# Routed cross attention: GpSimd's add of the normalised rows waits for the router's products, the second division goes ahead of the third maxima, the last copy ahead of an inverse

## The reference, cut to what matters

```python
qh, kh, vh = split(layernorm(x) @ wq + bq), split(ctx @ wk + bk), split(ctx @ wv + bv)
attn = softmax(einsum('bhqd,bhkd->bhqk', qh, kh) * scale)
x = x + (merge(einsum('bhqk,bhkd->bhqd', attn, vh)) @ wo + bo)
h = layernorm(x)
scores = h @ w_router            # one number for each token
_, idx = top_k(scores, 128)      # of the 512 tokens of the batch
x_sel = take(h, idx)             # goes to the mixture of depths
x = x + ffn(h)                   # ffn(h) is h, but for the chosen rows
```

## Time and profile before

| what | value |
| --- | --- |
| median of three runs (lowest, highest) | 2496.6 us (2495.58, 2496.82) |
| the profiled execution's own time | 2497.47 us |
| its span in the trace | 2495.6 us |
| TensorE busy | 91% of the span, 2259.5 us |
| VectorE, ScalarE, GpSimd busy | 57%, 48%, 30% |
| granted TensorE clock, mean | 0.963 of full speed |
| the stage of the change | about 505 to 815 us of the span |

### The profile page before, as it was taken

How to read it: one execution, slowest core, us unless ns; L and a number is a source line. 1 busy time by engine, 2 the same in 40 slices (tenths; PEclk the granted TensorE clock), 3 DMA queues, 4 the chain that set the end, 5 groups by cost and what they waited for, 6 DMA issues and landing times. The chain is left out here.

```text
span 2495.6 us, 44295 instructions
## 1 busy us (share of the span) xinstructions
PE 2259.5 (91%) x13992; PEld 1433.7 (57%) x13993; DVE 1423.5 (57%) x3651; ACT 1188.6 (48%) x2803; POOL 743.2 (30%) x848
## 2 busy tenths in 40 slices
PE   7999999888886699899999999889985899999998
PEld 5444554454555476643333333255552799999997
DVE  4666666435776354387777777366654534344343
ACT  1666666623432464258777777523322533333332
POOL 3112111043431331233232232054520533333333
PEclk8999999989998899999999999999997899999999
DMA  5343443113221320223333333010009322222221
GB/s 161 103 132 122 132 128 121 60 47 127 72 79 51 83 71 1 70 78 107 94 108 100 99 99 105 33 45 12 9 1 337 102 34 36 35 35 37 33 36 23
DMA packets 160823, 197.00 MB, mean 79 GB/s; under 512 B 27238, under 2 KB 121104, under 8 KB 160528
## 3 DMA queue, kind: packets, MB, share of 16 engines
q1 hardware_dynamic: 145008, 175.47, 22.6%
q0 software_dynamic: 13680, 17.84, 4.4%
q10 hardware_dynamic: 1968, 1.60, 0.4%
HBM read 124.83 MB, written 70.12 MB: 78 GB/s over the span
## 5 line engine op out<-in xcount | busy, mean ns | idle before, releaser
L485 ACT ACTIVATE self_probs<-self_score_ps 128x512 f32<-128x512 f32 (+3 forms) x1024 | 479.5, 516 | 260.1 <-PE self_score_ps L856 150.0
L653 DVE TENSOR_REDUCE self_neg_max<-self_max_ps 128x1 f32<-128x512 f32 x512 | 328.5, 685 | 127.7 <-PE self_max_ps L842 123.9
L842 PE MATMUL self_max_ps<-self_k_stack,self_q_stack 96*128 96x512 bf16 (+3 forms) x1024 | 349.1, 343 | 32.1 <-DVE self_neg_max L650 21.9
L853 PE MATMUL self_score_ps<-self_q_stack,self_k_stack 99*128 99x512 bf16 (+3 forms) x1024 | 345.9, 345 | 14.0 <-ACT self_probs L485 13.7
L2757 ACT ACTIVATE x_stream<-experts_up_ps,experts_bias_now 128x128 f32<-128x128 f32 x568 | 161.9, 368 | 351.0 <-PE experts_up_ps L2969 351.0
L650 DVE CUSTOM_DVE_ANT_0 self_masked<-self_max_ps,self_later 128x128 f32<-128x128 f32 (+3 forms) x512 | 235.0, 488 | 127.7 <-PE self_max_ps L842 120.3
L2969 PEld LDWEIGHTS experts_up_ps<-experts_tileT,x_stream 128*128 128x128 f32 x2272 | 266.8, 193 | 5.2 <-issue 1.6
L2969 PE MATMUL experts_up_ps<-experts_tileT,x_stream 128*128 128x128 f32 x2272 | 267.2, 276 | 1.2 <-DVE x_stream L2879 1.2
L2979 PE MATMUL experts_down_ps<-experts_down,x_stream 128*128 x1136 | 256.8, 379 | 0.0
L853 PEld LDWEIGHTS self_score_ps<-self_q_stack,self_k_stack 99*128 99x128 bf16 x1024 | 99.2, 98 | 248.3 <-ACT self_probs L485 181.4
L867 PE MATMUL self_out_ps<-self_probs,self_values 128*32 128x512 f32 (+3 forms) x2048 | 234.7, 530 | 7.3 <-ACT self_o_raw L471 5.4
(11 more groups left out here) (339 smaller groups left out, 3811.5 us busy)
## 6 DMA issues: line engine op xcount, KB each, us to landing
self_parts_dram<-self_parts SPq DMA_DIRECT2D x64, 384.0 KB, 2.7
self_q_stack<-self_parts_dram SPq DMA_DIRECT2D x384, 64.0 KB, 2.3
self_k_stack<-self_parts_dram SPq DMA_DIRECT2D x360, 64.0 KB, 2.3
self_out_dram<-self_o_raw SPq DMA_DIRECT2D x60, 256.0 KB, 2.2
crossx_out_dram<-crossx_o_raw SPq DMA_DIRECT2D x16, 512.0 KB, 2.7
experts_up<-moe_up_dram SPq DMA_DIRECT2D x8, 1024.0 KB, 9.3
experts_down<-moe_down_dram SPq DMA_DIRECT2D x8, 1024.0 KB, 10.6
self_o_now<-self_out_dram SPq DMA_DIRECT2D x30, 256.0 KB
```

Source lines behind the costliest of these rows:

```text
L485: act.activation(probs[:, i % 8, 0:w], score_ps[:, (16 * n + i) % 3, 0:w], ACT.Exp).then_inc(exp_done, 1)
L653: dve.tensor_reduce(neg_max[:, n % 2, t, h:h + 1], max_ps[:, i % 2, 0:w], AX, ALU.max, negate=True).then_inc(max_read, 1)
L842: last = pe.matmul(max_ps[:, i % 2, 0:w], q_stack[0:ROWS, h, P * t:P * t + P], k_stack[0:ROWS, h, 0:w], start=True, stop=True)
L853: last = pe.matmul(score_ps[:, m % 3, 0:w], k_stack[0:KROWS, head, P * j:P * j + P], q_stack[0:KROWS, head, S - w:S], start=True, stop=not ...
```

## The change

Three edits in the same stage, which change no arithmetic.

GpSimd's add x = x + h of a batch waits, beside h itself (`h_done`), for the four products with the router's row (`scored`). In each pass of ScalarE the inverse of the sums (b-1,1) goes ahead of the copy of the queries (b+2,1), and in each pass of VectorE the division (b-1,1), which needs this inverse, goes ahead of the maxima (b+1,2). After the loop, ScalarE copies out the last half (7,1) before it inverts the sums of (7,0), which wait for a load.

```diff
--- before.py
+++ after.py
@@ -1601,6 +1601,7 @@
                     pool.wait_ge(r_ln_eps, b + 1)
                     pool.tensor_tensor(r_rstd[:], r_var_eps[:], c.minus_half[:, 0:TT], ALU.pow).then_inc(r_ln_rstd, 1)
                     pool.wait_ge(h_done, TT * b + TT)
+                    pool.wait_ge(scored, TT * b + TT)
                     pool.tensor_tensor(c.x[:, b], c.x[:, b], h[:], ALU.add).then_inc(h_added, 1)
 
                 inverse_deviation(0)
@@ -1719,16 +1720,16 @@
                     if next2:
                         queries(b + 2, 0)
                     exponentials(b, 2)
+                    if b >= 1:
+                        inverted(b - 1, 1)
                     if next2:
                         queries(b + 2, 1)
-                    if b >= 1:
-                        inverted(b - 1, 1)
                     copy_out(b, 0)
                     exponentials(b, 3)
                     if b >= 2:
                         chosen_kept(b - 2)
+                copy_out(B - 1, 1)
                 inverted(B - 1, 0)
-                copy_out(B - 1, 1)
                 scores_copied(B - 2)
                 inverted(B - 1, 1)
                 chosen_kept(B - 2)
@@ -1863,10 +1864,10 @@
                         normalise(b - 1, 0)
                     if choice:
                         compare(b - 2, (0, 1))
+                    if b >= 1:
+                        normalise(b - 1, 1)
                     if more:
                         maxima(b + 1, 2)
-                    if b >= 1:
-                        normalise(b - 1, 1)
                     if choice:
                         compare(b - 2, (2, 3))
                         choose(b - 2)
```

## The result

The kernel with all three edits takes 2478.18 us (median of 5, 2473.38 to 2482.36), the one before on the same chip 2495.58 (median of 5, 2492.61 to 2496.82): a ratio of 0.993, 95% interval 0.9916 to 0.9945. The profiled execution took 2478.18 with a span of 2476.3, against a span of 2495.6 before.

What follows compares the result with a forecast made beforehand. TensorE was taken to bound the program, waiting at sr and e and losing clock. Batches 1 to 7 give 1.0, 0, 4.2, 6.0, 4.5, -1.45, 1.0, tail 4.0: 19.25 us, 2496.6 to 2477.6, range 2474 to 2486.

Steps and rivals of the forecast that it cites:

- rival 1: TensorE's clock doesn't come back and it stays partly at half clock; gain 13.5 us, 2483 us; 16 in 100.
- Rival 2: GpSimd's add, copy and bias add run as one 6.9 us piece, blocking VectorE's first division; 2483.5 us; 12 in 100.
- Rival 3: VectorE's second product is slow for its own reason; only the earlier division works; 2492 us; 4 in 100.
- rival 4: Load sets e in batches 3 to 5, merged idle piece costs half clock, 1.7 us each; 2498 us; 3 in 100.
- The stall: VectorE's second router product loses 2.15 us beside GpSimd's add in each of eight batches; holding the add ends it.
- The clock's part: TensorE's slow stretch behind sr in batches 3 to 5 returns to full clock: 5.7 us, bounded by 0 and 5.7.
- Where the stall goes: The add moves beside VectorE's next maxima, first division and comparisons; VectorE wins only 0.6 us in batch 5.
- The division: Moved forward on VectorE, it ends e's 1.00 us wait in batches 1, 3, 4, 5; gives 0.9 in batch 5.
- Pass 2: The gain at sr is waited away at e for a late load: 0 us, bounds -0.5 and 0.3.
- Pass 6: Load sets e; one idle piece of 3.65 us costs half clock: -1.45 us, bounds -1.7 and +0.25.
- Pass 7 and the tail: 1.0 us from batch 7's wait at e, plus 1.85 + 2.15 = 4.0 in the tail.
- Edit 3: Last half's store and loads leave about 3.7 us earlier; worth 0 by itself, 0.3 at most as cover.

Runs made afterwards that it cites:

- run 1: Kernel before with only GpSimd's add of x and h held until the router's products are done; 2482.61 us, ratio 0.9954.
- run 4: Kernel before with GpSimd's add of x and h replaced by a fill of an unused tile; one execution 2480.72 us, stage 237.25.
- run 5: Changed kernel with the inverse back ahead of the last copy, so without the third edit; 2481.68 us, ratio 0.9961.
- run 2: Kernel before with only the second inverse and division moved forward; 2490.01 us, ratio 0.9989.
- run 3: Kernel before with only the last copy put ahead of the inverse; one execution 2487.40 us, stage 250.46.
- run 7: Changed kernel with the next stage's weight loads spread over passes 1 to 6 and their scaling in pass 7; 2474.23 us, ratio 0.9917.
- run 9: Changed kernel with useless TensorE products ahead of e, 30 in pass 2 and 13 in passes 6 and 7, more in the tail; 2468.11 us, ratio 0.988.
- run 6: Changed kernel with useless TensorE products ahead of e, 56 in pass 2 and 24 in passes 6 and 7, more in the tail; 2480.13 us, ratio 0.9931.
- run 11: Changed kernel with 13 useless products in passes 6 and 7, the tail's, and weight loads behind half 0's store in passes 1 to 3; 2465.94 us, ratio 0.9883.
- run 10: Changed kernel with weight loads in passes 1 to 5 and 13 useless products in passes 6 and 7, plus the tail's; 2470.96 us, ratio 0.9897.

## Why the prediction was right

2477.6 was predicted and 2478.18 measured, in the range, with the forecast's own mechanism; rivals 1 to 4 didn't come. But the agreement to 0.6 is luck: the stage gave 16.66 where the sum had 19.25, while 3.57 were gained behind the stage and 0.93 lost ahead of it, where no edit reaches.

**The stall (edit 1): right.** A slow product needed GpSimd's add beside it, shown by run 1 (waits instead) and run 4 (fill instead), both with 424 ns at most. Rival 3 falls with run 4. The clock's part in passes 3 to 5, taken in full, came in full: the granted clock is 1.00 in all three, and run 1 gives 12.23 us in them, wait and clock together, for the 11.9 predicted. The 0.1 more in each pass is the full-clock time from sr to the scores of S, 3.14 for the 3.25 assumed. In these passes rival 1 falls.

**Where the stall goes: right in pass 5.** Division 1.56, ties 1.30 and 1.64 (as before the change), VectorE in at the hand-overs; the comparisons ended 7.3 us behind the products, 7.6 by the prediction. Rival 2's one piece of 6.9 didn't form. The sign given for it, a division near 2, fits passes 2 and 4 (1.99 and 1.83) better than 3 and 5 (1.56 both). That "the price is moved and not removed" was too dark: 17.0 us of stall became 6.6. Run 5 shows the other side of the rule: when GpSimd is 0.03 us ahead, the division pays the whole add.

**The division (edit 2): right.** 1.04, 1.04 and 0.75 in passes 3 to 5 for 0.9, 1.0 and 0.9. In pass 1 it gave 1.03 by run 2 (27.46 for 28.49, and the same 9.88 from S(1,0) to the scores of S(1,1), so the same clock); the 2.12 of the kernel after is 0.51 of this wait and 1.6 of the clock, which run 3 showed to vary there by as much. In pass 5 the load decided by the 0.25 shown above, its inverse 4.95 us behind its issue for 4.74, which is the meeting within 0.4 us that was forecast.

**Pass 2: right in kind.** -0.55 for 0, just past the bound of -0.5 and within what this pass varies by (run 3). The gain at sr is waited away at e, as said; run 7 shows that the weights ahead of the store are the reason.

**Pass 6: right in kind, its size off in this profile.** e is set by the load: it starts 15.82 us into the pass, 15.85 before, so the edits gave 0.03 where I took 0.25. Timelines of ScalarE and TensorE, for the earlier trace rows:

```profile
718.42 0.63 ACT L1675 ACTIVATE crossx_sums<-crossx_sums 128x512 f32<-128x512 f32 x1 [2.75 <-DMA crossx_sums<-crossx_out_dram]
...
720.59 3.75 PE L1933 MATMUL crossx_general<-crossx_wo,crossx_o_now 128*128 128x256 f32 x8 [3.90 <-DVE crossx_o_now L1781]
724.13 1.91 PE L1977 MATMUL crossx_score_ps<-ident,crossx_shifts 128*128 128x128 f32 x8
725.98 1.42 PE L1982 MATMUL crossx_score_ps<-crossx_q,crossx_k_blocks 32*128 32x512 f32 x4
727.32 1.13 PE L1965 MATMUL crossx_max_ps<-crossx_k_blocks,crossx_q 64*128 64x256 f32 x8
```

The idle piece is 3.90 (3.65 forecast), e 3.75 (3.1 forecast), and the half clock lasts through e, the transposes of S and part of the scores: from e to M it is 727.32 - 720.59 = 6.73, at full clock 3.83. The loss is 2.9 for the 1.7 that I had read off pass 2. In run 5 and in runs 1 and 4 (which lack edit 2) the same pass is 26.95, 27.30 and 27.07, which is 1.40 to 1.75 over before. So -1.45 was a fair value and -2.88 lies at the far end of what this pass does; my bound of -1.7 came from one row and was too near.

**Pass 7 and the tail: mis-sized**, 2.91 for 5.0. I counted 1.0 for the second division and 1.85 + 2.15 for the choices, and no clock. The waits came nearly as counted. From the pass's begin to e it is 0.88 us less (1.0 counted; luck in part, since e waits for the load there now, and in run 5, whose code is the same up to this point, it is 0.03), from bk of pass 7 to sr of batch 6 2.14 less and from there to bk of batch 6 0.06 more (together 2.08 for 1.85), and from the end of e in the tail to sr of batch 7 2.15 less (2.15 counted). But the time saved ahead of e of pass 7 again became one idle piece (3.64 instead of 1.23), and the work from e to bk took 0.94 longer at the lower clock; in the tail bk of batch 6 to e took 4.30 for 3.62 and e itself 4.45 for 3.62. These are 0.94 + 0.68 + 0.83 = 2.45, more than the 2.09 that the sum lacked; 0.26 came back between sr and bk of batch 7, the rest in the waits. So the term that was mis-sized is the clock behind e in pass 7 and the tail, put at nothing in the sum; it measured 2.45. Run 9, with the same dependencies and TensorE kept busy, gets 5.22 back in this stretch, more than these 2.45, since the kernel before ran part of it at half clock already (bk to e in the tail 3.62, 2.19 in run 9). The condition was known from pass 6 and wasn't applied to the passes after it.

**Edit 3: right at 0 alone, open beside the others.** Run 3 shows 0. Beside the others it stands between 0 and 1.0, by the turn of run 5, which neither the prediction nor my expectation of run 5 had. The nine kernels in the table there show that the load's duration decides the turn; whether edit 3 has a part in it stays open.

## What to carry to other kernels

Sum waits and clock by pass, and ask for each saved wait whether its time becomes work or one longer idle piece somewhere later: where the next wait is for a transfer with a date of its own, the saving is lost and the clock can go with it. Useless products in such a piece are cheap once their real duration is measured. A stall between VectorE and GpSimd shrinks when the long instruction runs beside one that it doesn't stop, here the maxima; only what is left is dealt to other instructions, so put that where the engine that then pays has slack. Compare these others with their durations before, or a stall that was always there is taken for the price. And beware of two instructions released within some hundredths of a us of each other.

## What the runs showed of the hardware that was not expected

- The order of two engines' instructions some hundredths of a us apart decides between 0.69 and 2.88 us for a division with two SBUF inputs: 0.02 ahead of GpSimd's add in run 9, 0.03 behind it in runs 5, 6 and 11.
- A load of 256 KB from DRAM that is issued at the same point of the tail reaches its first use on ScalarE after 4.62 to 5.25 us, from kernel to kernel.
- TensorE after one idle piece of 3.6 to 3.9 us lost 1.4 to 2.9 us to the half clock in pass 6, the same code from run to run; behind 3.17 us of filler and a piece of 1.93 it lost none (run 9), behind filler and 2.52 it did (run 10, e 3.49), and in run 11 behind 1.93 in part (e 3.11 in pass 7). Without filler, e of pass 2 ran at full clock (1.97) behind a piece of 2.58 in run 3.
- A product of the identity, fp32 128x128, takes 0.23 us and shows as two records (13 of them: 26 records, 3.17 us).
- A 512 KB store behind 3.3 MB of loads, issued in the 7 us before it on the same queue, had its load issued 9.26 us later instead of 2.76.
